# Storing expert results in slot order and gathering them per token, in two of three routed FFNs of a graph network

## What is computed

```
# layer 0 (called m0): 8 experts, best 2, hidden 256, gelu; plus the token itself
for e in range(E):
    h = gelu(tokens @ w1[e] + b1[e]);  y = h @ w2[e] + b2[e]
    out = out + combine[:, e:e + 1] * y
# layer 1 (m1): 32 experts, best 1, hidden 64, relu both times
# layer 3 (m3): 16 experts, best 2, hidden 512, relu, softmax of the best two
```

## Time and profile before

| | us |
|---|---|
| median of 3 timed runs | 3770.47 |
| lowest and highest | 3769.88, 3776.72 |
| the profiled execution, its own time | 3811.88 |
| span of the profiled execution | 3810.1 |
| TensorE busy | 2952.3 (77%) |
| GpSimd busy | 1710.0 (45%) |
| VectorE busy | 1266.4 (33%) |
| ScalarE busy | 790.4 (21%) |

### The profile page before, as it was taken

The page is one execution under the profiler, slowest core; times in us unless marked ns, Lnnn a source line. Parts: engine busy times, 40 slices in busy tenths (PEclk is TensorE's granted clock), DMA queues, the critical chain, the costliest instruction groups (busy, mean ns, idle before and its releaser), DMA issues. The chain is left out here.

```text
span 3810.1 us, 42840 instructions
## 1 busy us (share of the span) xinstructions
PE 2952.3 (77%) x12854; PEld 1734.1 (46%) x12855; DVE 1266.4 (33%) x4207; ACT 790.4 (21%) x1979; POOL 1710.0 (45%) x1277
## 2 busy tenths in 40 slices
PE   2344387888998484999899848699959589985992
PEld 1122133334445463444444534344449545564981
DVE  8899901202455524000300153400131410034116
ACT  4899800000001112100100011100023310011223
POOL 3888788836811266870581026486000120002554
PEclk9999998999998687999999855599969889977996
DMA  7889795778982355996798234599500054415994
GB/s 271 287 277 291 216 304 138 217 235 289 283 261 74 124 169 168 344 259 216 255 281 260 96 115 125 149 357 271 185 26 0 3 168 128 127 52 196 342 337 149
DMA packets 424684, 766.21 MB, mean 201 GB/s; under 512 B 158015, under 2 KB 270145, under 8 KB 414548
## 3 DMA queue, kind: packets, MB, share of 16 engines
q1 hardware_dynamic: 294548, 717.01, 53.7%
q0 software_dynamic: 129984, 47.34, 10.5%
HBM read 604.33 MB, written 159.84 MB: 201 GB/s over the span
## 5 line engine op out<-in xcount | busy, mean ns | idle before, releaser
L793 PE MATMUL sum_psum<-abuf,y 128*128 128x512 f32 (+1 forms) x3500 | 1420.9, 566 | 191.3 <-ACT y L716 129.0
L793 PEld LDWEIGHTS sum_psum<-abuf,y 128*128 128x128 f32 x3500 | 628.8, 191 | 963.3 <-issue 895.8
L554 POOL DMA_INDIRECT table_t<-sums,index_from x392 | 617.0, 1574 | 356.2 <-POOLq L2017 132.4
L554 POOL DMA_INDIRECT table_pairs<-sums,index_to x392 | 611.1, 1559 | 190.3 <-issue 120.4
L726 ACT ACTIVATE gathered<-sum_psum 128x512 f32<-128x512 f32 (+1 forms) x84 | 41.0, 540 | 1773.0 <-PE sum_psum L793 1773.0
L793 PE MATMUL sum_psum<-abuf,acc 128*128 128x512 f32 (+1 forms) x700 | 285.6, 568 | 9.4 <-DMA abuf<-table_pairs 9.4
L1510 PE MATMUL m_x_hp<-m_x_xt,m_x_wa 128*128 128x128 f32 (+1 forms) x1720 | 264.3, 307 | 36.5 <-issue 7.7
L1496 PE MATMUL m_x_yp<-m_x_wb,m_x_h 128*128 128x256 f32 (+2 forms) x860 | 260.5, 437 | 38.7 <-ACT m_x_h L1539 33.9
L1446 POOL DMA_INDIRECT results<-m_x_yo,land_i x178 | 175.2, 984 | 255.4 <-DVE m_x_yo L1561 175.3
L434 PE MATMUL merge_psum<-part,acc 128*128 128x6 bf16 x980 | 71.0, 167 | 241.9 <-DVE pass_on L508 137.3
L1510 PEld LDWEIGHTS m_x_hp<-m_x_xt,m_x_wa 128*128 128x128 f32 (+1 forms) x1720 | 229.2, 205 | 62.1 <-issue 36.7
(11 more groups left out here) (359 smaller groups left out, 2982.4 us busy)
## 6 DMA issues: line engine op xcount, KB each, us to landing
abuf<-table_pairs SPq DMA_DIRECT2D x750, 512.0 KB
table_pairs<-zero SPq DMA_DIRECT2D x50, 1600.0 KB
table_t<-zero SPq DMA_DIRECT2D x25, 1600.0 KB
abuf<-table_t SPq DMA_DIRECT2D x150, 256.0 KB
m_x_wa<-in_L_ffn_w_dram SPq DMA_DIRECT2D x65, 512.0 KB
m_x_wb<-in_L_ffn_w_dram SPq DMA_DIRECT2D x65, 512.0 KB
abuf<-table_pairs SPq DMA_DIRECT2D x125, 128.0 KB
m_x_rows<-results SPq DMA_DIRECT2D x25, 640.0 KB, 9.3
```

The costliest lines, as they stand in the source:

```text
L554: nc.gpsimd.indirect_dma_start(table[:, :], bass.IndirectOffsetOnAxis(ap=index[:, g, j:j + 1], axis=0), k.sums[:, g, j, 0:width], None, co ...
L793: mm = nc.tensor.matmul(k.sum_psum[:, b % 2, f, 0:n], h[:, c, f * P:(f + 1) * P], operand(i % ring, c - q * QUART, n), start=(c == 0), sto ...
```

## The change

In m0 and m1 (`in_order`, where the hidden size is at most 256) the expert results are stored to `results` in slot order: ScalarE, behind the activation of every second tile, waits for the results of two tiles and issues one plain transfer of 256 rows; two semaphores `stored` take the place of the four `landed`. The scatters go. In `combine`, GpSimd waits for the stores and gathers the rows of each token tile and choice from `results` by `slot_i`, 50 indirect transfers in m0 and 25 in m1, each 128 rows of 1 KB, with the joins of m0 among them, five tiles behind. SyncE no longer reads there. m3 keeps its scatters and plain reads. The diff is whole, but for unchanged surroundings:

```diff
@@ -1403,9 +1403,11 @@
     loaded = [sem(f"{m.name}_x_loaded{u}") for u in range(W)]
     rows_in = [sem(f"{m.name}_x_rows_in{u}") for u in range(2 * DEEP)]
     landed = [sem(f"{m.name}_x_landed{u}") for u in range(DEEP)]
+    stored = [sem(f"{m.name}_x_stored{u}") for u in range(2)]
     b2_in = sem(f"{m.name}_x_b2_in")
     rows_b1 = E * FB
     ROUND = 2 * DEEP
+    in_order = m.F <= 256
 
     def experts_from(engine, c):
 
@@ -1440,13 +1442,13 @@
                         nc.gpsimd.indirect_dma_start(xin[:, c % ROUND, :], None, tokens,
                                                      bass.IndirectOffsetOnAxis(ap=k.gather_i[:, c:c + 1], axis=0))\
                             .then_inc(rows_in[c % ROUND], 16)
-                    if c >= GATHERED:
+                    if c >= GATHERED and not in_order:
                         d = c - GATHERED
                         pool.wait_ge(s["out"], d + 1)
                         nc.gpsimd.indirect_dma_start(results,
                                                      bass.IndirectOffsetOnAxis(ap=k.land_i[:, d:d + 1], axis=0),
                                                      yo[:, d % DEEP, :], None).then_inc(landed[d % DEEP], 16)
-                for u in range(DEEP):
+                for u in range(0 if in_order else DEEP):
                     pool.wait_ge(landed[u], 16 * len(range(u, n, DEEP)))
 
             @block.sync
@@ -1528,6 +1530,11 @@
                 act.wait_ge(s["b1"], 1)
                 experts = []
 
+                def store(c, u, count):
+                    act.wait_ge(s["out"], c + count)
+                    act.dma_start(results[bass.ds(c * P, count * P), :].rearrange("(t p) f -> p t f", p=P),
+                                  yo[:, u:u + count, :]).then_inc(stored[u // 2], 16)
+
                 def step(c, u, i, first):
                     if u % DEEP == 0:
                         experts[:] = experts_from(mybir.EngineType.Activation, c)
@@ -1539,7 +1546,13 @@
                         ins = nc.scalar.activation(h[:, u % 2, f, :], h_psum[:, u % 2, f * P:(f + 1) * P], func,
                                                    bias=b1t[:, bass.ds(e * FB + f, 1)])
                     ins.then_inc(s["hidden"], 1)
+
+                    if in_order and u % 2 and (not first or u > 2):
+                        store(c - 3, (u - 3) % DEEP, 2)
                 over(act, n, ROUND, step)
+                if in_order:
+                    for c in range(n - 2 - n % 2, n, 2):
+                        store(c, c % DEEP, min(2, n - c))
 
             @block.vector
             def _(dve):
@@ -1556,7 +1569,10 @@
                     dve.wait_ge(s["down"], c + 1)
                     if not isinstance(c, int) or c >= DEEP:
 
-                        dve.wait_ge(landed[u % DEEP], (2 * i + u // DEEP) * 16)
+                        if in_order:
+                            dve.wait_ge(stored[u % DEEP // 2], (2 * i + u // DEEP) * 16)
+                        else:
+                            dve.wait_ge(landed[u % DEEP], (2 * i + u // DEEP) * 16)
                     to = yo[:, u % DEEP, :]
                     ins = nc.vector.tensor_tensor(to, y_psum[:, u % 2, 0:D],
                                                   b2b[:, bass.ds(e, 1), :].rearrange("p e f -> p (e f)"), ALU.add)
@@ -1580,18 +1596,25 @@
                 dve.wait_ge(b2_in, 16)
                 over(dve, n, ROUND, step, last_apart=True)
                 finish(n - 1, (n - 1) % ROUND, (n - 1) // ROUND, experts_from(mybir.EngineType.DVE, n - 1)[0])
-            combine(nc, k, m, block, rows, results, into, weighted, landed, roots)
-
-
-def combine(nc, k, m, block, rows, results, into, weighted, landed, roots):
+            combine(nc, k, m, block, rows, results, into, weighted, landed, stored if in_order else None, roots)
+
+
+def combine(nc, k, m, block, rows, results, into, weighted, landed, stored, roots):
 
 
     n, K = m.tiles, m.K
     came = [k.sem(f"{m.name}_c_came{u}") for u in range(TILES // AHEAD)]
     weighed, joined, added = (k.sem(f"{m.name}_c_{v}") for v in ("weighed", "joined", "added"))
 
+    def join(pool, t):
+        pool.wait_ge(weighed, t + 1)
+        nc.gpsimd.tensor_tensor(rows[:, 1, t, :], rows[:, 1, t, :], into[:, t, :], ALU.add).then_inc(joined, 1)
+    whole = 16 * K * (AHEAD if stored is not None else 1)
+
     @block.sync
     def _(sp):
+        if stored is not None:
+            return
         for u in range(DEEP):
             sp.wait_ge(landed[u], 16 * len(range(u, n, DEEP)))
         for t in range(0, TILES, AHEAD):
@@ -1599,6 +1622,23 @@
                 at = j * NP + t * P
                 sp.dma_start(rows[:, j, t:t + AHEAD, :], results[at:at + AHEAD * P, :].rearrange("(t p) f -> p t f", p=P))\
                     .then_inc(came[t // AHEAD], 16)
+
+    @block.gpsimd
+    def _(pool):
+        if stored is None:
+            return
+        for u in range(2):
+            pool.wait_ge(stored[u], 16 * len(range(2 * u, n, DEEP)))
+        for t in range(TILES):
+            for j in range(K):
+                nc.gpsimd.indirect_dma_start(rows[:, j, t, :], None, results[0:n * P, :],
+                                             bass.IndirectOffsetOnAxis(ap=k.slot_i[:, K * t + j:K * t + j + 1], axis=0))\
+                    .then_inc(came[t // AHEAD], 16)
+            if weighted and t >= AHEAD:
+                join(pool, t - AHEAD)
+        for t in range(TILES - AHEAD, TILES):
+            if weighted:
+                join(pool, t)
     if roots:
         degree_roots(nc, k, block)
 
@@ -1606,21 +1646,21 @@
         @block.scalar
         def _(act):
             for t in range(TILES):
-                act.wait_ge(came[t // AHEAD], 16 * K)
+                act.wait_ge(came[t // AHEAD], whole)
                 nc.scalar.activation(rows[:, 1, t, :], rows[:, 1, t, :], ACT.Copy, scale=k.choice[:, 2 * t + 1:2 * t + 2])\
                     .then_inc(weighed, 1)
 
         @block.gpsimd
         def _(pool):
-            for t in range(TILES):
-                pool.wait_ge(weighed, t + 1)
-                nc.gpsimd.tensor_tensor(rows[:, 1, t, :], rows[:, 1, t, :], into[:, t, :], ALU.add).then_inc(joined, 1)
+            if stored is None:
+                for t in range(TILES):
+                    join(pool, t)
 
     @block.vector
     def _(dve):
         for t in range(TILES + 1):
             if t < TILES:
-                dve.wait_ge(came[t // AHEAD], 16 * K)
+                dve.wait_ge(came[t // AHEAD], whole)
                 if weighted:
                     dve.wait_ge(joined, t + 1)
                     nc.vector.scalar_tensor_tensor(into[:, t, :], rows[:, 0, t, :], k.choice[:, 2 * t:2 * t + 1],
```

## The result

The changed kernel takes 3831.45 us (median of 4 runs, 3828.83 to 3836.03) against 3773.59 (4 runs, 3769.88 to 3780.99) for the kernel before: ratio 1.0152, 95% interval 1.0132 to 1.0173. That is 57.9 us slower, where +24 was forecast. The direction is right and the time lies at the upper edge of the range, but the size is more than twice the forecast, so the working has to be opened.

The account below looks back on a forecast made before the run. It took m0's loop as bound by GpSimd's issue plus pauses, m1's by TensorE at its low clock. Terms -43 - 11 + 61 + 17 = +24 us on the 3770.5 median gave 3794.5 us, range 3770 to 3832.

Parts of the forecast that it names:

- 2.58 is GpSimd's issue and 0.44 these pauses: m0 loop before: 3.02 us a step, split into GpSimd's gather and scatter issue and recurring waits when its queue is full.
- Term 1: m0 loop: without scatters on GpSimd a step falls from 3.02 to 2.25 us, -43 us.
- Term 2: m1 loop: bound by TensorE at its low clock, 55 steps of 2.84 us against 167.2 us, -11 us.
- Term 3: m0 tail: 50 gathers on GpSimd with joins and waits between, 96.2 us against 34.5, +61 us.
- Term 4: m1 tail: gathers on GpSimd with most sums hidden beside them, 41.1 us against 23.9, +17 us.
- The pauses belong to the profiled execution alone: m0 and m1 loops: timed runs lack the pauses, so loops gain only 18 and 0 us; +60, 3830 us; chance 0.18.
- Landing becomes the wait: m0 loop: stores land late and VectorE waits once in two tiles; gain 21 instead of 43, 3816 us; chance 0.08.
- The clock of m1: m1 loop: TensorE might be granted 2.4 GHz without pauses, 46 us more saved, 3748 us; chance 0.08.

Follow-up runs that it names:

- e1: The kernel before, run again with nothing changed, on a chip with pauses: 3820.39 us.
- e11: The kernel before, unchanged, profiled on a chip of the other kind, without pauses: 3773.53 us.
- e5: The changed kernel again, beside the kernel before on one chip with pauses: 3828.86 against 3825.64 us, ratio 1.0010.
- e6: The changed kernel with m0's tail joins moved from GpSimd to VectorE and ScalarE's scaling gone: 3819.58 us against the changed kernel's 3828.86.

## Why the prediction was right in sign and wrong in size

The step that failed is the division of 3.02 us a step, "2.58 is GpSimd's issue and 0.44 these pauses", together with the sum's base: the four terms were worked out on a trace with pauses and then put on a median that had none. The record doesn't name the chips of the first comparison, but by times and missing records the profile of the kernel before came from a chip with pauses (3811.9; e1's chip gave 3808 to 3825), and its timed runs, by their times, from one without (3770; e11's gave 3767 to 3779). The 41 us between the two numbers was in front of me. It should have carried the forecast, or at least half the chance: a trace that is 41 us longer than the runs it stands for holds 41 us that a change can't save in them.

Term by term, with what each measured on either kind of chip (from the table: e5 against e1, and the kernel after against e11):

```
                 forecast   with pauses    without
m0 loop            -43         -51.8        -18.9
m1 loop            -11         -16.0          0.0
m0 tail            +61         +49.9        +49.3
m1 tail            +17         +16.0        +15.8
sum                +24          -1.9        +46.2
timed               -           +3.2        +57.9
```

So the right sign hung on where the runs were timed: on a chip with pauses the change makes no difference that the runs can tell. And without pauses the savings were put 35 us too high and the tails 13 us too high, so that part of the error cancelled.

- **Term 1** is right in kind: GpSimd stands idle before each gather and TensorE sets the pace, 120.0/56 = 2.14 us a step where 2.25 was taken. Its base was wrong: without pauses the loop before lasts 138.9 us, 2.48 a step. That is below GpSimd's 2.58 a tile, since seven of the gathers are issued before the first result and one scatter after the last (106 instructions in the window, not 114).
- **Term 2**: 153.0 us whether GpSimd scatters or not, once there are no pauses. TensorE at a granted clock of 0.50 is the only limit.
- **Term 3** is 12 us too high. The gathers run at 1.26 us start to start, not 1.29 (1.5 us over 49 steps). A gather, a join and the next gather take 1.86, so a join adds 0.6 and not 0.95 (6.6 us over 19 joins). GpSimd never waits for a group between the gathers (2.8 us), and the first gather starts 2.0 us behind the last result instead of 3.3 (1.3). The joins' median fell from 902 ns to 732. VectorE now seldom works beside them: the 22 joins with little or none of its sums beside take 724 to 740 ns, the last three, with a sum and statistics beside each, 902 to 915. (A sum beside isn't always felt: the second join of the kernel before has 572 ns of one beside it and takes 717.) The Trainium skill (GPSIMD Engine Reference, section Key points) says that GpSimd shares its SBUF interfaces with VectorE; the trace agrees, with 170 ns on a join, more than the 5% that I read off the index transfers.
- **Term 4** holds: 40.2 us where 41.1 was worked out.
- **A term was missing**, some 5 us ("behind" is 734.3 against 729.2): the barrier behind the tail. GpSimd's drain at the end of the block, in the kernel after and in e11 (ns, start):

```profile
L1435 POOLq DRAIN  x1: 11273/11273/11273, 1518.5 to 1518.5; - x1
```
```profile
L1433 POOLq DRAIN  x1: 6612/6612/6612, 1482.7 to 1482.7; - x1
```

The last statistics end at 1522.6, and the drain only at 1518.5 + 11.3 = 1529.8; the next stage's first instruction on VectorE starts another 1.2 us later. In e11 the drain ends at 1489.3 with the statistics at 1489.2. The timeline of the kernel after:

```profile
1521.87 0.74 DVE L1672 BATCH_NORM_STATS2 stats<-x 128x6 f32<-128x256 f32 x2
...
1530.94 0.08 DVE L576 MEMSET ln_work<- 128x25 f32 x1 [8.34 <-PEq L1899]
```

In e6, where the gathers end 11 us before the statistics, the drain is covered and "behind" is 730.4 again, 4 us less. I wrote that the next layer begins only after the block ends, and counted the block as ended with its last statistics.

The rest of the 57.9 lies in m1's lead (25.6 to 26.1 against 22.6, 25.4 or more in each run with m1 in slot order and 23.6 at most in the others; why was not tried), in m0's lead (22.2 against 20.2) and in stages that the change doesn't touch: m0's first gather starts 1290 to 1300 us into the span, whatever the kernel.

**The rivals.** "The pauses belong to the profiled execution alone" forecast 3830 and loops of -18 and 0, and 3831, -18.9 and 0.0 were measured. Its numbers are right and its reason is not: e1's timed runs have the pauses' time and e11's profile has no pauses. What decides is the chip or something that holds for a whole visit to it, not which execution is profiled. It had a chance of 0.18 for the match of 37 and 41 us alone. "Landing becomes the wait" didn't happen (1.8 us in all) until a second gather was added. The clock of m1 stayed at 0.50 in every run, also in e11, where TensorE is busy 152.0 of 153.0 us. The Trainium skill (TensorE: Matmul & The Clock Gate, section Part 1) would have a dense stream released to the full clock; the measurement decides against it here.

## What to carry to other kernels

Before a sum is put on a median, compare the profiled execution's own time with it: a gap of 41 us against an uncertainty of 7.5 is a finding, to be placed before anything else is worked out. A saving measured in waits that no instruction explains must be shown to exist in the runs that are timed. And work moved behind a loop is paid in full, drain and barrier included, while the engine it leaves gives back only what it really limited: here 19 us against 49 in m0, and 0 against 16 in m1.

## What was not expected of the hardware

- Chips differ by kernel. The kernel before takes 3816 to 3826 us on three chips (0, 4, 5) and 3768 to 3774 on four (1, 3, 11, 12), with the same instructions. The changed kernel takes 3829 on one of the first kind (5) and 3831 in the first comparison. No chip was visited twice, and the three visits with pauses came before the four without, so chip and time of visit aren't told apart; the first comparison, ahead of them all, has both kinds. The difference is the pauses, in loops where GpSimd issues two indirect DMAs a step of 2 to 3 us; m3, which has two in 3.7 us, takes 244.0 us in e1 and 244.7 in e11.
- GpSimd's drain at a block's end, after row gathers, ends 8.8 us after its last join (1518.49 + 11.27 against 1520.9), where it ends 1.8 us after it without gathers in the tail (e11). It is no matter of the joins: in e6, without any, the drain ends 8.8 us after the last gather's row. The Trainium skill (Perfetto Trace Analysis, section DMA Instruction — SWDGE (GPSIMD)) says that the profile's end of such an instruction is the end of descriptor generation and not of the data's movement. The trace agrees: in the tails a gather takes 0.95 us by its row and lands 2.7 to 2.8 us after its start. Neither explains a drain of 8.8.
- The page of the kernel after has a mean granted clock of 0.826, lower in its first slices, and its other runs 0.884 to 0.885; it is the fastest of the four. So that mean says nothing of the time here.
